# Last rows' remainders on VectorE, the last sum and store in column halves, and the shared expert's down step in two stacked products

## What is computed

```
x = x + attention(pooled(x))                 # conditioned pooling, latent attention with rotary, per sequence
h = x @ W[cat] + b[cat]                      # one of 64 matrices per sequence
w = route(h)                                 # top 8 of 64 experts in the 4 best groups, weights scaled by 2.5
y = sum over e of w[:, e] * (silu(h @ Wg[e]) * (h @ Wu[e])) @ Wd[e]      # 64 experts, inner width 64, computed densely
shared = (silu(h @ Ws_gate) * (h @ Ws_up)) @ Ws_down                     # inner width 64
out = x + y + shared
```

## Time and profile before

| | |
|---|---|
| median of 3 plain runs | 723.68 us (723.67 to 724.1) |
| profiled execution | 725.9 us, its span 724.0 us |
| granted TensorE clock, mean | 0.992 of full speed |
| instructions | 15734 |
| busy: matmul / VectorE / ScalarE / GpSimd | 96% / 75% / 61% / 59% |

### The profile page before, as it was taken

One profiled execution on the slowest core, in us unless ns is written; L12 is line 12 of the kernel. 1 busy time (PEld: TensorE's weight loads), 2 busy tenths in 40 slices (PEclk: granted clock), 3 DMA queues, 4 the chain that ended last, 5 costly groups with the idle time before them and its releaser, 6 DMA issues.

```text
span 724.0 us, 15734 instructions
## 1 busy us (share of the span) xinstructions
PE 697.4 (96%) x5606; PEld 544.1 (75%) x5606; DVE 544.5 (75%) x1146; ACT 442.7 (61%) x857; POOL 425.6 (59%) x351
## 2 busy tenths in 40 slices
PE   7878899899999999999999999999999999999997
PEld 5656677677887778777787778877787777887885
DVE  5777669686697787887688865976878876886664
ACT  3865865477555865478455675558654685565554
POOL 3626696865555655566455654566455664666665
PEclk9989999999999999999999999999999999999999
DMA  8272554345344445435544464444465344355441
GB/s 269 75 285 81 154 131 117 89 123 154 104 130 111 139 106 130 138 101 155 116 110 131 117 149 109 127 114 143 107 126 144 92 146 123 108 127 146 129 131 45
DMA packets 65117, 92.93 MB, mean 128 GB/s; under 512 B 7696, under 2 KB 26576, under 8 KB 65040
## 3 DMA queue, kind: packets, MB, share of 16 engines
q1 hardware_dynamic: 61008, 87.06, 44.5%
q10 hardware_dynamic: 4032, 4.87, 1.9%
HBM read 88.37 MB, written 3.15 MB: 126 GB/s over the span
## 4 chain that ended last, share of the span: by engine, by line
PE 70%; ACT 8%; DVE 8%; SPq 6%; issue 4%; DMA 2%; POOL 1%; POOLq 0%; DVEq 0%
PE banks L1026 68%; DVE hid L984 2%; SPq L316 2%; SPq L310 2%; ACT banks L543 2%; ACT s_t L424 2%; DVE hid L1002 2%; PE banks L1108 1%; ACT L543 1%; DVE k_blk L710 1%; ACT hid_hi L555 1%; ACT L424 1%; DMA gbias<-in_gate_bias 1%; DVE pt_sb L685 1%; POOL hid_lo L657 1%
## 5 line engine op out<-in xcount | busy, mean ns | idle before, releaser
L657 POOL TENSOR_TENSOR hid_lo<-hid,hid_hi 128x512 fp32r<-128x512 f32 (+1 forms) x264 | 343.3, 1300 | 255.8 <-ACT hid_hi L555 253.9
L984 DVE TENSOR_TENSOR hid<-banks,cwb 128x512 f32<-128x512 f32 x252 | 173.2, 687 | 117.1 <-ACT banks L543 114.4
L543 ACT ACTIVATE banks<-banks 128x512 f32<-128x512 f32 x252 | 146.1, 582 | 129.6 <-PE banks L1026 127.9
L555 ACT CAST hid_hi<-hid 128x512 fp32r<-128x512 f32 (+1 forms) x264 | 162.6, 616 | 79.3 <-DVE hid L1002 78.6
L1002 DVE TENSOR_TENSOR hid<-hid,banks 128x512 f32<-128x512 f32 (+1 forms) x262 | 180.0, 687 | 27.9 <-PE banks L1026 5.8
L1026 PE MATMUL banks<-c_hi,wg_hi 128*128 128x512 f32 x264 | 119.0, 451 | 5.6 <-POOL wu_lo L622 2.3
L1026 PE MATMUL banks<-hid_hi,wd_hi 128*128 128x512 f32 (+1 forms) x264 | 104.6, 396 | 0.8 <-POOL hid_lo L657 0.8
L1026 PE MATMUL banks<-c_hi,wu_hi 128*128 128x512 f32 x256 | 102.0, 398 | 2.3 <-DVE hid L1002 2.3
L1026 PE MATMUL banks<-c_hi,wg_lo 128*128 128x512 f32 x264 | 103.5, 392 | 0.0
L1026 PE MATMUL banks<-c_lo,wg_hi 128*128 128x512 f32 x264 | 103.5, 392 | 0.0
L1026 PE MATMUL banks<-hid_lo,wd_hi 128*128 128x512 f32 (+1 forms) x264 | 103.4, 392 | 0.0
(11 more groups left out here) (160 smaller groups left out, 799.6 us busy)
## 6 DMA issues: line engine op xcount, KB each, us to landing
cwb<-cw_scratch SPq DMA_DIRECT2D x254, 256.0 KB, 3.8
k_blk<-in_cond_w SPq DMA_DIRECT2D x112, 64.0 KB
xf<-in_x_feat SPq DMA_DIRECT2D x8, 256.0 KB, 4.0
out_feat<-y ACTq DMA_DIRECT2D x8, 256.0 KB, 3.6
wg_raw<-in_we_gate SPq DMA_DIRECT2D x3, 512.0 KB, 7.5
wu_raw<-in_we_up SPq DMA_DIRECT2D x3, 512.0 KB, 8.0
wd_raw<-in_we_down SPq DMA_DIRECT2D x3, 512.0 KB, 9.4
xf<-in_x_tok SPq DMA_DIRECT2D x6, 256.0 KB, 2.8
```

The source lines that it names most:

```text
L543: nc.scalar.activation(dst, gate_bank(p)[:, :], ACT.Silu).then_inc(S["silu_done"], 1)
L555: nc.scalar.copy(hid_hi[0:n, slot(b, p), :], hid[0:n, slot(b, p), :]).then_inc(S["hi_ready"], 1)
L657: nc.gpsimd.tensor_sub(hid_lo[0:n, slot(b, p), :], hid[0:n, slot(b, p), :], hid_hi[0:n, slot(b, p), :].bitcast(F32)).then_inc(S["lo_ready" ...
L984: nc.vector.tensor_mul(hid[:, slot(b, p), :], gate_bank(p)[:, :], cwb[:, p % NCW, :])\
```

## The change

- Of the last block, VectorE (`last_rests`) instead of GpSimd makes the remainders of units 31 and 32. GpSimd's `unit` returns before them.
- The last sum is two VectorE additions of 256 columns each. ACT stores the first half, SP the second.
- In every block the remainder of the shared expert's 64 hidden rows goes into partitions 64 to 127 of its `hid_hi` buffer, below the rounded rows in 0 to 63. The rounded down weights stand twice, in partitions 0 to 63 and 64 to 127 (SP loads them twice, ACT rounds all 128 partitions). The down step of unit 32 is then one product of 128 rows, which does high with high and high with low at once, and one of 64 rows, low with high: two instead of three.
- GpSimd waits for its own previous remainder ahead of units 32 and 0.

```
--- before.py
+++ after.py
@@ -333,7 +333,8 @@
                 for m in range(2):
                     weight_load(k, m)
             sp.dma_start(wg_raw[:, NPAIR, :], ws_gu).then_inc(S["ws_in"], 16)
-            sp.dma_start(wd_raw[0:F, NPAIR, :], ws_down).then_inc(S["ws_in"], 16)
+            for i in range(2):
+                sp.dma_start(wd_raw[F * i:F * i + F, NPAIR, :], ws_down).then_inc(S["ws_in"], 16)
             sp.wait_ge(S["c2tok_ps"], 1)
             for k in (2, 3):
                 weight_load(k, 2)
@@ -359,7 +360,9 @@
                     sp.dma_start(cwb[:, p % NCW, :], src).then_inc(cwb_in[p % NCW], 16)
 
             pipeline(unit_loads)
-            sp.wait_ge(S["y_free"], 16 * NBLK + 16)
+            sp.wait_ge(S["y_ready"], NBLK + 2)
+            sp.dma_start(out[:, bass.ts(2 * NBLK - 1, TOK // 2)], y[:, TOK // 2:TOK]).then_inc(S["y_free"], 16)
+            sp.wait_ge(S["y_free"], 16 * NBLK + 32)
 
 
         @block.scalar
@@ -469,9 +472,9 @@
                     hi, lo, raw = half_tile(i)
                     nc.scalar.copy(hi, raw).then_inc(S["split_hi"], 1)
                 else:
-                    act.wait_ge(S["ws_in"], 32)
+                    act.wait_ge(S["ws_in"], 48)
                     nc.scalar.copy(wg_hi[:, NPAIR, :], wg_raw[:, NPAIR, :])
-                    nc.scalar.copy(wd_hi[0:F, NPAIR, :], wd_raw[0:F, NPAIR, :]).then_inc(S["split_hi"], 1)
+                    nc.scalar.copy(wd_hi[:, NPAIR, :], wd_raw[:, NPAIR, :]).then_inc(S["split_hi"], 1)
 
             act.dma_start(c[:, :], consts).then_inc(S["consts_in"], 16)
             act.sem_inc(S["y_free"], 16)
@@ -592,7 +595,7 @@
             pipeline(unit)
             rounded(NBLK - 1, UNITS - 1)
             act.wait_ge(S["y_ready"], NBLK + 1)
-            act.dma_start(out[:, bass.ts(NBLK - 1, TOK)], y[:, :]).then_inc(S["y_free"], 16)
+            act.dma_start(out[:, bass.ts(2 * NBLK - 2, TOK // 2)], y[:, 0:TOK // 2]).then_inc(S["y_free"], 16)
 
 
         @block.gpsimd
@@ -652,9 +655,14 @@
                 split(i)
 
             def unit(b, p, par, following, last, prev):
+                if b == NBLK - 1 and p >= NPAIR - 1:
+                    return
                 pool.wait_ge(S["hi_ready"], b * UNITS + p + 1)
                 n = P if p < NPAIR else F
-                nc.gpsimd.tensor_sub(hid_lo[0:n, slot(b, p), :], hid[0:n, slot(b, p), :],
+                if p == NPAIR or (p == 0 and b):
+                    pool.wait_ge(S["lo_ready"], b * UNITS + p)
+                rest = hid_lo[:, slot(b, p), :] if p < NPAIR else hid_hi[F:2 * F, slot(b, p), :]
+                nc.gpsimd.tensor_sub(rest, hid[0:n, slot(b, p), :],
                                      hid_hi[0:n, slot(b, p), :].bitcast(F32)).then_inc(S["lo_ready"], 1)
                 if not prev and p in SPLITS:
                     split(SPLITS[p])
@@ -1012,10 +1020,26 @@
                     if step == LOW:
                         rest_of_input(blk, 1 - par)
 
+            def last_rests():
+
+                dve.wait_ge(S["hid_ready"], NBLK * UNITS)
+                for p in range(NPAIR - 1, UNITS):
+                    n = P if p < NPAIR else F
+                    at = slot(NBLK - 1, p)
+                    rest = hid_lo[:, at, :] if p < NPAIR else hid_hi[F:2 * F, at, :]
+                    dve.wait_ge(S["hi_ready"], (NBLK - 1) * UNITS + p + 1)
+                    dve.wait_ge(S["lo_ready"], (NBLK - 1) * UNITS + p)
+                    nc.vector.tensor_sub(rest, hid[0:n, at, :], hid_hi[0:n, at, :].bitcast(F32)).then_inc(S["lo_ready"], 1)
+
             gate_up(0)
             gate_up(1)
             pipeline(unit)
-            total(NBLK - 1)
+            last_rests()
+            dve.wait_ge(S["down_done"], NBLK * UNITS)
+            dve.wait_ge(S["x2_moved"], NBLK)
+            for i in range(2):
+                part = bass.ts(i, TOK // 2)
+                nc.vector.tensor_add(y[:, part], Y[:, part], y[:, part]).then_inc(S["y_ready"], 1)
 
 
         @block.tensor
@@ -1269,7 +1293,6 @@
                 return mm(dst, w_hi, m_lo, start=False, stop=final)
 
             def down(b, p):
-                n = P if p < NPAIR else F
                 pe.wait_ge(S["lo_ready"], b * UNITS + p + 1)
                 if b == 0 and p % 4 == 0:
                     pe.wait_ge(S["split_lo"], 3 * (p // 4) + 3 if p < NPAIR else NSPLIT + 1)
@@ -1277,8 +1300,13 @@
                     if b == 0:
                         pe.wait_ge(S["weighted"], NPAIR + 1)
                     pe.wait_ge(S["y_ready"], b + 1)
-                three(Y[:, :], wd_hi[0:n, p, :], wd_lo[0:n, p, :], hid_hi[0:n, slot(b, p), :], hid_lo[0:n, slot(b, p), :],
-                      p == 0, p == UNITS - 1).then_inc(S["down_done"], 1)
+                if p == NPAIR:
+                    mm(Y[:, :], wd_hi[:, p, :], hid_hi[:, slot(b, p), :], start=False, stop=False)
+                    last = mm(Y[:, :], wd_lo[0:F, p, :], hid_hi[0:F, slot(b, p), :], start=False, stop=True)
+                else:
+                    last = three(Y[:, :], wd_hi[:, p, :], wd_lo[:, p, :], hid_hi[:, slot(b, p), :], hid_lo[:, slot(b, p), :],
+                                 p == 0, False)
+                last.then_inc(S["down_done"], 1)
 
             def gate(b, p, par, following):
                 if b == 0 and p % 4 == 0:
```

## The result

| | before | after |
|---|---|---|
| median | 723.67 us | 720.57 us |
| profiled execution: span | 724.0 us | 718.7 us |
| granted TensorE clock, mean | 0.992 | 0.997 |

The medians differ by 3.1 us, 0.4%. The ratio of the times is 0.9953, interval [0.9935, 0.9972], which is 2.0 to 4.7 us. The forecast was 721.4 with 720.6 to 722.6. One of the nine launches of the changed kernel took 1131.93 us at a granted clock of 0.557; the ratio leaves it out, and without it the median is 720.40.

What follows compares the result with a forecast made beforehand. TensorE, busy 96% of the 724.0 us span, was taken to bound the kernel where it sets the pace. Tail 0.95 plus boundaries 1.37 make 2.32 us: 723.68 - 2.32 = 721.4, range 720.6 to 722.6.

Steps and rivals of the forecast that it cites:

- Subtractions: In the tail, VectorE's two subtractions of 0.69 us each finish the last remainder 0.66 us earlier than GpSimd did.
- Products and sum: In the tail, unit 32's products end 0.68 us earlier, the shape change taking 0.20; splitting the sum costs 0.06.
- Store: At the end, half stores from ACT and SP land at 722.6; the whole tail is 0.95 us shorter.
- Boundaries: Each of seven block boundaries drops one product: six give 0.19 us each, one 0.23, together 1.37.
- The seventh: The block boundary without attention work, where TensorE alone sets the pace: the dropped product gives 0.23 us.
- What costs nothing: GpSimd's new waits, some 0.1 us each, and the second weight load, 0.54 us of SP's queue, are covered.
- (a): Rival: of the block boundaries only the seventh gives; gain 1.18 us, time 722.5; chance 0.15.
- (b): Rival: in the tail GpSimd's work stretches both moved subtractions by 1.9 us, leaving 0.4: 723.3; chance 0.05.
- (c): Rival: all seven boundaries give 0.228 us and the tail 1.2, together 2.8: 720.9; chance 0.11.
- (d): Rival: within blocks VectorE's operations meet GpSimd's more often, 0.96 us each; 3.5 slower, 727.2; chance 0.05.
- How the numbers follow: Chances for the whole time: forecast 0.64; faster 0.78, same 0.19, slower 0.03; range 720.6 to 722.6 us.
- The sum of 2.32: Whole gain in us: 0.95 in the tail plus 1.37 at the seven block boundaries.

Runs made afterwards that it cites:

- padded: Changed kernel with the low half of the shared down weights over all 128 partitions, no 64-row product left; 3.49 ± 0.65 us less than the kernel before, ratio 0.995.
- tail_only: Changed kernel with the stacking taken back, so unit 32 has three 64-row products again; ratio 1.001 to the kernel before, tail 6.35 us.
- one_load: Changed kernel with the shared down weights loaded once, ACT writing the rounded form into both halves in two operations; median 720.88 us.
- collide: Changed kernel with GpSimd kept busy by three scratch subtractions beside VectorE's last two remainders; tail 7.92 us instead of 6.22, span 723.7.

## Why the prediction was nearly right, and where it failed

**Subtractions.** Forecast: first rest ready 1.50 after the start of unit 32's product; it was 713.21 + 0.69 - 712.48 = 1.42. The gap after VectorE's own previous result was 0.04 (712.48 + 0.69 to 713.21), not 0.12; that two of its three waits had been met by then may be why, but is not shown. The second gap was 0.10, forecast 0.11. Writing into the other partitions costs nothing: 0.69 as the first.

**Products and sum.** Unit 32's load 0.05 after the rest; the sum began 0.97 after that load, and TensorE's two products took, as forecast, 0.93 by the profile's modelled end (715.18 + 0.49 = 715.67, load at 714.74). The 0.43 at the shape change was exact. The tail came out at 6.22, and padded, without the shape change, at 6.03 and 6.01, so a change costs 0.2 us here. The load itself takes 0.18 with 64 rows and 0.19 with 128. The Trainium skill says in "TensorEngine Tiling (Array Packing)", Key Properties, that changing the tiling mode drains TensorE; this trace agrees. That rows do not matter for a weight load, as the Trainium skill says in "TensorE: Matmul & The Clock Gate", Step-by-step: what each phase is for, holds for the load by itself; as the only rule it would have given a tail of about 6.0. The prediction's sum holds without a word on one thing: the stacking also takes the shape change ahead of unit 32 off the path, which is worth 0.10 once VectorE makes the remainders (tail_only, whose expectation of 6.2 to 6.3 missed it by 0.05).

**Store.** ACT issued at +3.68 and SP at +4.01, forecast 3.78 and 4.11. From SP's issue to the end it was 2.21, forecast 2.11. The halves moved up to 343 GB/s together, the whole one up to 399, in slices of different length. Early by 0.10, late by 0.10: the tail came to 6.22, 0.95 less, as forecast.

**Boundaries.** Five periods gained 1.02, 0.20 each, forecast 0.19. ACT's rounding starts 0.03 behind VectorE's product (242.04 + 0.69 to 242.76), forecast 0.04. ACT's silu just ahead of it waits for TensorE; the rounding started 0.49 after that silu's start in the kernel before (245.48 to 245.97) and 0.54 after it now (242.22 to 242.76). So VectorE's product holds it up by the 0.05 that turn 0.25 into 0.20, and padded, where the rounding waits 0.35 for VectorE, shows that a further product's worth would not have helped. The seventh gained 102.76 - 102.43 = 0.33 where 0.23 was forecast; 0.25 is in the products themselves. From the last gate product of that unit to the first of the next it was 658.07 - 656.06 = 2.01 and is 653.73 - 651.97 = 1.76. Six boundaries together: 1.35, with a forecast of 5 x 0.19 + 0.23 = 1.18. Middle and tail together give 2.30; with the first boundary's 0.17 it is 2.47 in the span, and less the 0.2 outside the span about 2.25 in time.

**What costs nothing** cost nothing that can be seen: one_load for the second load; for GpSimd's waits the idle time of 2.48 behind them. What the prediction did not say is that the same wait costs 0.14 wherever GpSimd's pair is exposed, which the change avoids by moving the pair.

**The rivals.** (a) fell by the five periods. (b) didn't occur, and collide shows that it would have with GpSimd busy. (c) came in half: its 1.59 for seven boundaries was nearly met (1.35 and 0.17), its 1.2 for the tail was not. (d), collisions between the blocks, fell: the middle is shorter by more than was forecast.

**The step that failed** is "How the numbers follow": the range. It was made of the bounds of the costs, 720.6 to 722.6, and left out that the time itself has a spread. Three plain runs of before within 0.43 us suggested none; 35 later ones had a standard deviation of 2.0, and the profiled execution, 2.2 above their median, had been a hint. A median of nine such runs is uncertain by about 1.25 x 2.0 / 3 = 0.8, an estimate for a bell-shaped spread, and 720.57 is 0.8 below the forecast. The sum of 2.32 stands inside 2.5 ± 0.4. That it comes this close is in part luck: in the traces the terms add up to 2.47, 0.15 more than the sum, and the 0.2 outside the span, which the prediction put at nothing by taking the span's difference off the median, goes the other way. The extra gain of the first series is most likely chance of the opening: of the 5.3 us between the two profiled spans, 3.0 lay ahead of the first piece of 115 products, 0.17 of it the change's, and the rest goes with falls of the clock that either kernel has or lacks.

## What to carry to other kernels

Compare two kernels between milestones that both traces have, and look at how far a stretch that the edit does not touch scatters before calling a gain of half a per cent the edit's; three plain runs do not show that. Put the low half of a split operand below its high half where rows are free: it takes out one product of three, but see that no other engine's unbroken run decides there. Short work of GpSimd at the end of a kernel goes to VectorE with profit, as long as GpSimd is then truly idle.

## What was not expected of the hardware

- **The clock does not fall every time.** Behind the same 2.3 us of idle time the granted clock fell in eleven traces and not in one, to 0.50 (a mean of 0.83 from 130 to 140), and a fall costs about 1.1 us. What decides it is not shown. Over the 195 runs of the three later series, one thousandth less of mean granted clock goes with 0.33 ± 0.04 us more time, whichever kernel.
- **The same kernel's opening moves by 2.9 us** (before, 133.92 and 131.02) or 4.2 (padded, 130.25 and 134.40), later where the clock fell before 80 us.
- **Contention costs both sides**: a VectorE subtraction beside GpSimd's goes from 0.69 to 1.5 to 1.65, GpSimd's from 1.30 to 1.5 to 1.7 in collide (in the earlier trace rows the one of 1.30 beside it was not longer; spans on GpSimd are rough).
- **Two stores on two queues** are hardly better than one whole store behind a whole sum: 2.22 from the later issue instead of 2.44, although it is half the size.
